# Statistics of z taken by bn_stats on the vector engine instead of Square with an accumulator on the scalar engine

## The reference, cut to what matters

```
x = x + LN( attn( LN(x) ) )        # first half
x = x + LN( ffn( LN(x) ) )         # second half,  LN(x) = (x - mean) / sqrt(var + 1e-5)

attn(u):  o = causal_conv(u, K) + D * u         # K[c,t] = C[c] * sigmoid(A[c])**t * B[c], length 256
          z = u + gelu(o) @ W_proj.T + b_proj
          return (z - mean(z)) * rsqrt(var(z) + 1e-5) * gamma + beta

ffn(v):   vp = v shifted by one token
          r = sigmoid((mu_r*v + (1-mu_r)*vp) @ W_r.T);  k = (mu_k*v + (1-mu_k)*vp) @ W_k.T
          return r * (square(relu(k)) @ W_v.T)
```

## Time and profile before

| | |
|---|---|
| median of 3 runs | 192.52 us (192.18 to 192.86) |
| the profiled execution | 192.55 us, of it 190.8 us span |
| instructions | 3481 |
| busy share of the span | PE 75%, DVE 73%, ACT 74%, POOL 71% |
| read and written | 4.79 MB and 4.19 MB |

### The profile page before, as it was taken

How to read it: one execution, slowest core, us unless ns; L and a number is a source line. 1 busy time by engine, 2 the same in 40 slices (tenths; PEclk the granted TensorE clock), 3 DMA queues, 4 the chain that set the end, 5 groups by cost and what they waited for, 6 DMA issues and landing times.

```text
span 190.8 us, 3481 instructions
## 1 busy us (share of the span) xinstructions
PE 143.0 (75%) x904; PEld 117.5 (62%) x904; DVE 140.2 (73%) x400; ACT 141.7 (74%) x420; POOL 136.2 (71%) x140
## 2 busy tenths in 40 slices
PE   0074961675689997998999899979989969879300
PEld 0052860664658794987679587949877746757200
DVE  0736049979998699999989898979989899331400
ACT  3371664076669588989998998999896996969360
POOL 3450326694983985999999989999996997743551
PEclk9999699579889999999999999999999999999955
DMA  4789700000000000000300030021003004030213
GB/s 119 187 224 273 200 0 2 2 0 3 0 0 0 5 0 0 3 3 0 110 0 3 4 108 0 0 71 39 0 0 112 0 2 115 0 110 0 63 47 110
DMA packets 18670, 9.14 MB, mean 48 GB/s; under 512 B 1120, under 2 KB 18656, under 8 KB 18656
## 3 DMA queue, kind: packets, MB, share of 16 engines
q1 hardware_dynamic: 17936, 8.98, 17.2%
q10 hardware_dynamic: 720, 0.00, 0.2%
HBM read 4.79 MB, written 4.19 MB: 47 GB/s over the span
## 4 chain that ended last, share of the span: by engine, by line
PE 38%; ACT 25%; DVE 16%; issue 9%; POOL 5%; DMA 2%; ACTq 1%; POOLq 1%; DVEq 0%
ACT f_normal L360 8%; PE ps_prefix L662 7%; PE ps_z L681 7%; ACT t_scaled L370 5%; ACT xn L325 5%; PE ps_prefix L664 3%; PE ps_r L714 3%; PE ps_r L713 3%; DVE y L513 3%; PE ps_xT L653 3%; PE ps_z L682 3%; PE ps_k L702 3%; DVE conv_scaled L496 3%; DMA x_all<-in_x 2%; ACT junk L350 2%
## 5 line engine op out<-in xcount | busy, mean ns | idle before, releaser
L360 ACT ACTIVATE f_normal<-f,out_bias,sf_r 128x128 f32<-128x128 f32 x64 | 26.1, 480 | 4.6 <-POOL out_bias L264 4.6
L325 ACT ACTIVATE xn<-x_all,x_bias,sx_r 128x128 f32<-128x128 f32 (+1 forms) x64 | 26.2, 489 | 3.7 <-POOL x_bias L212 3.7
L681 PE MATMUL ps_z<-pv_T,gelu 128*128 128x128 f32 x128 | 25.1, 298 | 4.3 <-DVE y L513 4.3
L221 POOL TENSOR_TENSOR xn_pow<-xn,pow_token 128x512 f32<-128x512 f32 x16 | 20.6, 1288 | 8.0 <-ACT xn L325 7.8
L270 POOL TENSOR_TENSOR x_all<-f_normal,x_all 128x512 f32<-128x512 f32 (+1 forms) x16 | 20.4, 1282 | 7.3 <-ACT f_normal L360 7.3
L714 PE MATMUL ps_r<-mixed_T,tsT 128*128 128x128 f32 x128 | 24.7, 275 | 0.0
L713 PE MATMUL ps_r<-mixed_T,tsT 128*128 128x128 f32 x128 | 24.7, 275 | 0.0
L681 PEld LDWEIGHTS ps_z<-pv_T,gelu 128*128 128x128 f32 x128 | 20.7, 204 | 5.8 <-issue 4.3
L522 DVE SCALAR_TENSOR_TENSOR x_all<-y,sy_r,x_all 128x128 f32<-128x128 f32 (+1 forms) x64 | 22.9, 418 | 1.2 <-POOL sy_r L245 1.1
L662 PE MATMUL ps_prefix<-prefix_ones,xn_pow 128*128 128x256 f32 x64 | 23.0, 446 | 0.3 <-POOL xn_pow L221 0.3
L350 ACT ACTIVATE junk<-ps_z 128x128 f32<-128x128 f32 x64 | 16.5, 273 | 8.9 <-PE ps_z L682 8.6
(11 more groups left out here) (79 smaller groups left out, 372.3 us busy)
## 6 DMA issues: line engine op xcount, KB each, us to landing
x_all<-in_x SPq DMA_DIRECT2D x8, 512.0 KB, 6.6
out_x<-x_all SPq DMA_DIRECT2D x8, 512.0 KB, 3.2
bias_row<-in_b_proj SPq DMA_DIRECT2D x1, 64.0 KB, 4.5
w_pv<-in_W_proj SPq DMA_DIRECT2D x1, 64.0 KB, 4.8
w_pv<-in_W_v SPq DMA_DIRECT2D x1, 64.0 KB, 4.9
gamma_row<-in_gamma SPq DMA_DIRECT2D x1, 64.0 KB, 6.3
beta_row<-in_beta SPq DMA_DIRECT2D x1, 64.0 KB, 8.5
w_rk<-in_W_r SPq DMA_DIRECT2D x1, 64.0 KB, 5.2
```

The costliest lines, as they stand in the source:

```text
L221: g_.tensor_tensor(xn_pow[h][:].rearrange("p (q l) -> p q l", l=SEQ), xn[h][:].rearrange("p (q l) -> p q l", l=SEQ), pow_token[:].rearrang ...
L325: last = a_.activation(tile(xn[h], j), xa(g, k), ACT.Identity, bias=x_bias[:, k:k + 1], scale=Sx["r"][:, k:k + 1])
L360: last = a_.activation(tile(f_normal[h], j), tile(f[h], j), ACT.Identity, bias=out_bias[:, k:k + 1], scale=Sf["r"][:, k:k + 1])
L681: t_.matmul(tile(ps_z[h], j), tile(gelu[h], j), pv_T[:, 0, :], start=True, stop=False)
```

## The change

ScalarE's `square_z` goes, and with it the buffers `junk`, `z_var` and `eps_tile`. VectorE gets `z_moments_of`: for each half it waits for the projection, runs two `bn_stats` straight from the bank `ps_z[h]`, and after the second half one 128x8 `tensor_scalar` that divides by 128 and adds eps. GpSimd's `z_scale_of` keeps only the power. In VectorE's body the first half of a group is taken after `convolve(g - 1, 1)`, the second half one body later, between `t_moments_of(g - 3, 0)` and `residual(g - 3, 1)`.

```diff
-        z_var = sb("z_var", TILES)
+        z_raw = sb("z_raw", TILES, 3)
...
-            g_.memset(eps_tile[:], EPS)
...
             def z_scale_of(g):
-                pool.wait_ge(z_squares, 2 * g + 2)
+                pool.wait_ge(z_moments, g + 1)
                 later(pool, y_scaled, 2 * g, g)
-                g_.tensor_tensor(z_ve[:], z_var[:], eps_tile[:], ALU.add).then_inc(pc["z"], 1)
-                pool.wait_ge(pc["z"], g + 1)
                 g_.tensor_tensor(z_r[:], z_ve[:], neg_half[:], ALU.pow).then_inc(z_scale, 1)
...
-            def square_z(g, h):
-
-                act.wait_ge(z_ready, 2 * g + h + 1)
-                later(act, z_scale, g, g)
-                for j in range(HALF):
-                    k = h * HALF + j
-                    last = a_.activation(tile(junk, k), tile(ps_z[h], j), ACT.Square, scale=float(P) ** -0.5,
-                                         accum_out=z_var[:, k:k + 1])
-                last.then_inc(z_squares, 1)
...
-                if runs(g, 1):
-                    square_z(g - 1, 0)
...
-                if runs(g, 1):
-                    square_z(g - 1, 1)
...
+            def z_moments_of(g, h):
+
+                dve.wait_ge(z_ready, 2 * g + h + 1)
+                for q in range(HALF // 2):
+                    k = h * HALF + 2 * q
+                    last = v_.bn_stats(z_raw[:, k:k + 2, :].rearrange("p i c -> p (i c)"),
+                                       two(ps_z[h], q).rearrange("p (i c) -> p c i", i=2))
+                if h == 1:
+                    last.then_inc(z_stats, 1)
+                    dve.wait_ge(z_stats, g + 1)
+                    later(dve, z_scale, g, g)
+                    v_.tensor_scalar(z_ve[:], z_raw[:, :, 2], 1.0 / P, EPS, ALU.mult, ALU.add).then_inc(z_moments, 1)
...
                 if runs(g, 3):
                     t_moments_of(g - 3, 0)
+                if runs(g, 2):
+                    z_moments_of(g - 2, 1)
                 if runs(g, 3):
                     residual(g - 3, 1)
...
                 if runs(g, 1):
                     convolve(g - 1, 1)
+                if runs(g, 1):
+                    z_moments_of(g - 1, 0)
                 if runs(g, 4):
                     gate(g - 4, 1)
```

More of the change, by code:

```diff
@@ L57, in sandwich @@
         neg_half = sb("neg_half", TILES)
-        eps_tile = sb("eps_tile", TILES)
         a_col = sb("a_col", 1)
@@ L96, in sandwich @@
         f_normal = [sb(f"f_normal{h}", HW) for h in range(2)]
-        junk = sb("junk", GW)
         def stats(name):
@@ L130, in sandwich @@
         z_ready, y_scaled, y_ready = sem("z_ready"), sem("y_scaled"), sem("y_ready")
-        z_squares, z_scale = sem("z_squares"), sem("z_scale")
+        z_stats, z_moments, z_scale = sem("z_stats"), sem("z_moments"), sem("z_scale")
         y_stats, y_moments, y_scale, t_ready = (sem(n) for n in ("y_stats", "y_moments", "y_scale", "t_ready"))
@@ L139, in sandwich @@
         stored = sem("stored")
-        pc = {n: sem(f"pool_{n}") for n in ("x", "z", "y", "shift", "f", "f_shift")}
+        pc = {n: sem(f"pool_{n}") for n in ("x", "y", "shift", "f", "f_shift")}
         block = ctx.enter_context(nc.Block())
```

## The result

The changed kernel takes 202.97 us (median of 4 runs, 202.44 to 203.85) where the kernel before takes 192.35 us (4 runs, 191.45 to 192.86): a ratio of 1.056, 95% interval 1.0505 to 1.0619. It is slower by 10.6 us, 2.5 us more than forecast, inside the range. The profiled execution took 203.85 us, 202.1 us of it span; before, 190.8 us.

What follows compares the result with a forecast made beforehand. Four engines were taken as tied, VectorE having at most 0.56 us of waiting a turn to give; 192.55 + 5.8 issue time + 2.5 collisions, less 0.1 us of ScalarE's relief in four turns, made 200.5 us, range 195.0 to 205.0.

Steps and rivals of the forecast that it cites:

- (a, b): To 41.9 us, added statistics fall into VectorE's prefix-sum waits: 0; from 41.9 to 47.2, VectorE nearly full: +1.5 us.
- (c): Stretch ending at 63.43: the earlier 1.5 us stays, new statistics fall into the 1.94 us wait: 0.
- (d): From 63.43 to 80.83, VectorE has no wait, so the added statistics cost +1.5 us.
- (e): Two full turns, 80.83 to 116.0, with 0.56 us of waiting to use up: +1.0 us each, 2.0 us.
- (f): Turn up to 133.56, with waits of 1.12 and 0.29 us to use up: +0.1 us.
- (g): Up to 150.14, with 0.85 us of waiting for z_r to use up: +0.7 us.
- The collisions: VectorE instructions held by GpSimd's 128x512 operations, mainly st_ve in five bodies: +2.5 us together, bounds -3 and +7.
- Second and third less the residual's gain: Over four turns, holds of sx_negmean and sy_ve less the first residual's vanished hold: 0, bounds -3 and +2 us.
- Rival A: VectorE binds but collisions do not grow, st_ve slipping in ahead of GpSimd: about 197.3 us, chance 0.23.
- Rival B: All collisions strike, or TensorE, idling more, gets the lower clock: 203.3 to 205.3 us, chance 0.13.
- C: Faster, ScalarE's relief decides, up to 1.0 us a turn: 188.5 us, partial case about 191 us; chance 0.06.
- D: No change, vanished collisions and a faster z_r making good the added time: 192.5 us, chance 0.06.

Runs made afterwards that it cites:

- 1: Kernel before plus 32 bn_stats on a constant table and 8 tensor_scalars on VectorE, results unused, squares kept on ScalarE: 201.70 us, ratio 1.0475.
- 5: Kernel before without the squares, variance of z a constant, nothing in their place: 191.08 us, ratio 0.9941.
- 2: Changed kernel without its 32 bn_stats of z, z_ve made at its place from a constant: 192.62 us, ratio 1.0024.
- 3: Changed kernel with t's scale ahead of the second xn_times_pow in GpSimd's body: 200.77 us, ratio 1.0363.
- 4: Changed kernel with the 128x8 operations on statistics of x, t and f moved from VectorE to ScalarE: 195.47 us, ratio 1.0135.
- 7: Kernel before with TensorE's transposes of t put ahead of a stage of values: 191.57 us, ratio 0.9964.
- 9: Changed kernel, bn_stats of z for groups 2 to 6 only, other groups' squares on ScalarE, x, t, f small operations there in full turns: 192.21 us, ratio 0.9966.
- 6: Changed kernel with x, t, f small operations on ScalarE and TensorE's transposes of t ahead of values: 193.44 us, ratio 1.0076.
- 8: Changed kernel, z statistics split between VectorE and ScalarE by group, full-turn small operations on ScalarE, TensorE's t transposes ahead of values: 189.29 us, ratio 0.9861.

## Why the prediction was right, and where its sum was not

The mechanism was the right one: VectorE becomes the bound, about half of the added 12 us hides in its waits, ScalarE's relief is nearly all off the path, and holds grow. The marks came as said: VectorE busy 157.1 us with the highest share, bn_stats from the bank 417 ns, turns of 19.2, 19.3, 19.4 and 18.7 us, no wait in the full turns. Stretch by stretch, with the holds taken out by start-to-start times:

| stretch of before | longer by | holds | the rest | the rest, predicted |
|---|---|---|---|---|
| start of the kernel to 23.69 | 0.93 | 0 | 0.93 | 0 |
| (a, b) to 47.17 | 2.44 | 0.90 | 1.54 | 1.5 |
| (c) to 63.43 | 1.70 | 0.51 | 1.19 | 0 |
| (d) to 80.83 | 1.79 | 0.39 | 1.40 | 1.5 |
| (e) to 115.98 | 3.57 | 2.85 | 0.72 | 2.0 |
| (f) to 133.56 | 1.16 | 1.20 | -0.04 | 0.1 |
| (g) to 150.14 | -0.39 | -0.29 | -0.10 | 0.7 |
| sum | 11.20 | 5.56 | 5.64 | 5.8 |

**Issue time.** 4.7 us without the first row, against 5.8 predicted. The small total error hides two larger ones. In (c) the statistics were to fall into the wait of 1.94 us. That wait is gone, but waits of 1.34 us (at 58.66) and 0.17 us stand elsewhere in the stretch. TensorE's prefix sums hang on VectorE and came later with it, and TensorE's clock had a part that the sum left out. In after it was granted 0.50, the lower of its two levels (1.2 GHz), from 51.7 to 58.5 us; TensorE had idled for 5.61 us up to 52.15. In before it was 0.50 from 50.7 to 54.1 us, after 3.19 us of idling up to 48.78. The stretch of after, and the four transposes of xn in it:

```profile
51.70:58.40 6.70, 6.25 (x24) 5.60 (x25) 5.55 (x19) 2.48 (x6) 5.66 (x6) 0.50 0.00 1
```

```profile
52.15 1.08 PE L651 MATMUL ps_xT<-ident,xn 128*128 128x128 f32 x4 [5.61 <-DVE conv L483]
```

The same four take 0.63 us at 48.78 in before, granted 1.00. The wait of 1.34 us ends with the last prefix sum of this stretch. That the change sent the clock down for longer is not shown: the executions of experiments 1 and 5 have 0.50 for 6.8 us there too, those of 2, 3 and 4 for 3.4 us. In (e) I counted 0.56 us a turn of waiting as cover and left out the 0.36 us put down to issue at the loop's edge, which a late VectorE does not have either; gaps of some 0.3 us in all around the small operations closed too.

**The collisions are the mis-sized term.** Predicted +2.5 us, measured +5.6 us. Summed over the stretches: st_ve +4.95, the residual -4.84, sf_negmean +3.80, wait_holder +1.06, x's pair +0.88, y's pair -0.29. st_ve was the step that failed. The prediction had it 0.1 to 0.3 us too late and took half of the hold, because the lead was thin. It came 0.23 us too late (106.01 against 105.78) in the turn shown, 0.18 to 0.24 us in all, and was held in six bodies (3 to 8), every one in which GpSimd still had a second product; the prediction had counted five. A lead worked out between two chains that both start at z_ve does not scatter: the thinness is no reason for half. The five bodies of the prediction in full, at its 1.0 us each, are 5.0 us, and the sum would have been 203.0 us, which is what was measured. That closeness is luck: the issue time came out 1.1 us lower, the other holds 0.6 us higher, and the start, which the change did not cause, adds 0.9 us.

"Second and third less the residual's gain" was taken as 0. It was -4.25 us, beyond its bound of -3: sx_negmean took 0.7 us a turn as said, the residual's hold went in every turn, and sy_ve was mostly free. But the prediction let the residual's hold vanish because VectorE would find GpSimd's first product over. VectorE was indeed elsewhere, at sf_negmean, and was held there for 3.80 us in all. This replacement was not in the forecast. Experiments 1 and 3 show the same: a hold that is taken from one instruction turns up at a neighbour.

**The start.** 0.93 us has arisen by 24.62 us; the first added instruction starts at 26.01. The rows are TensorE's, of after:

```profile
18.47 1.09 PE L651 MATMUL ps_xT<-ident,xn 128*128 128x128 f32 x4 [2.63 <-DVE conv L483]
```

and of before:

```profile
18.50 0.63 PE L653 MATMUL ps_xT<-ident,xn 128*128 128x128 f32 x4 [2.63 <-DVE conv L502]
```

Same work, same idle time ahead of it, 1.09 us against 0.63: the two durations that these transposes have at a granted clock of 0.50 and of 1.00, as in (c). The stretch's own row, with the granted clock as its last number but two, seems to say the opposite (first row after, second before).

```profile
18.40:24.00 5.60, 5.53 (x22) 5.25 (x23) 0.84 (x4) 2.92 (x6) 2.81 (x3) 1.00 0.82 208
```

```profile
18.40:24.00 5.60, 5.16 (x24) 4.44 (x24) 1.18 (x5) 3.96 (x14) 1.88 (x3) 0.70 0.77 204
```

But the first clock record in the trace of after is a rise to 1.00 at 24.35 us, in before one at 16.59 us, and a row shows 1.00 where there is no record. Read by the durations, TensorE stood at its lower level up to 24.35 us in after, while in before it was at the upper one from 16.59 us on, but for 20.0 to 23.4. The eleven profiled executions fall into two groups. In after and in numbers 3, 4, 5, 7 and 9 the first record is at 23.4 to 24.6 us, the transposes take 1.09 us, and the convolution that follows stands at 24.10 to 24.90. In before and in numbers 1, 2, 6 and 8 the first record is at 15.1 to 16.6 us, the transposes take 0.63 to 0.74 us, and the convolution stands at 23.18 to 23.69. Both groups hold kernels with the statistics on VectorE and without. So the first row goes with the execution, not with the change, and fits the profiled execution being 0.9 us above the median. What sends an execution into one group or the other is open.

**ScalarE.** The relief was credited with 0.4 us, experiment 5 has 1.1 us (0.3 to 1.9 by the interval), 0.17 us a turn. The direction was right and the size small either way. "Busy near 112 us" was wrong: 125.8. The 16.5 and 13.2 us of the earlier trace rows overlap; what leaves the engine is 15.9 us, the start-to-start figure of the prediction, and the mark should have been made from that one.

**The rivals.** Rival A, no growth of the holds, falls with the holds of every full turn; its own terms, 192.5 + 5.4, make 197.9 us and not 197.3. Rival B named 203.3 to 205.3 us and was largely right: nearly all holds struck, and TensorE's clock, though at 1.00 in the full turns, was at 0.50 for 6.8 us in (c), where before has 3.4 us. C and D fall with the result, and experiment 5 gives the reason: ScalarE's relief alone is worth 1.1 us.

**The two rules.** The bank's price from the Trainium skill, VectorE: DVE Perf Modes, section on the TRN2 errata, an estimated 65 ns more on each bn_stats, is not seen: 417 ns from the bank and 414 ns from SBUF over 32 each. The Trainium skill, SBUF — State Buffer, section Who interferes with whom, has whoever issues first block the other. The prediction set the residual of the earlier trace rows against it and misread the row: 92.69 is the start of a group of four instructions. Two took 0.35 us each; the held one is the third, and VectorE's list has it as

```profile
93.22 1.38 DVE L522 SCALAR_TENSOR_TENSOR x_all<-y,sy_r,x_all 128x128 f32 x1
```

behind GpSimd's start at 93.18. So the trace agrees. In before and after every held instruction began while a 128x512 operation of GpSimd was running, st_ve at 106.01 behind 105.78 among them. The other way round, GpSimd's product at 110.84 in before, which began 0.02 us behind an instruction of the residual, took 1.45 us instead of 1.27. What the prediction drew from its reading, about 3 us more by the rule, falls with it.

## What to carry to other kernels

When engines are tied, price a move by start-to-start times and by place: 16 us taken off ScalarE were worth 1 us, 12 us put on VectorE cost some 5 us and brought 5.6 us of holds with them, in the execution that was profiled. Find each small VectorE operation's place relative to GpSimd's large ones by the chain that starts both, and count a hold in full where the chain is fixed; expect a part of a hold that leaves one instruction at its neighbour. Look at the instructions of a group one by one before you say which engine was first, and see whether a row's clock is recorded or only filled in. Then divide such work by group: on the engine that has room in that phase of the pipeline, with the small operations off the engine that is held.

## What the runs showed of the hardware

- A tensor_scalar on 128x8, and a tensor_tensor with both inputs in SBUF on 128x1, that begin while a 128x512 operation of GpSimd runs are held for the whole rest of it, up to 1.2 us beyond their 0.08 us step. The second kind I had not expected. From VectorE's list of after:

```profile
62.55 1.21 DVE L470 TENSOR_TENSOR wait_holder<-d_col 128x1 f32<-128x1 f32 x1
```

- bn_stats from SBUF is not held: two in 0.76 us in the midst of two additions of GpSimd that run from 109.66 to 112.17, and only the sx_negmean behind them is long. VectorE's list, then GpSimd's:

```profile
110.53 0.76 DVE L443 BATCH_NORM_STATS2 sx_raw<-x_all 128x6 f32 x2
111.32 0.88 DVE L450 TENSOR_SCALAR sx_negmean<-sx_raw 128x8 f32<-128x8 f32 x1
```

```profile
109.66 2.51 POOL L233 TENSOR_TENSOR y<-y,beta_row 128x512 f32<-128x512 f32 x2 [0.87 <-DVE y L507]
```

- Square with an accumulator shows 273 and 207 ns busy for its two instructions, but the pair takes 0.25 us from start to start (four in 1.00 us).
